# A Mamba block and a router on one core: summing over states by transposes that add in PSUM, with the gate turned instead of the output

## What is computed

```
x  = einsum(ctx, in_proj_w);  u = silu(causal_conv4(x) + conv_b)
dt_low, B, C = split(x_proj_w @ u);  dt = softplus(dt_proj_w @ dt_low + dt_proj_b)
state = state * exp(dt * A) + (dt * u) * B        # step by step over 1024 tokens
y  = sum over 16 states (state * C) + D * u
y  = y * silu(z),  z = layernorm(x), seen as (channel, token)
x2 = x + tanh(g_xattn) * transpose(y)
out = x2 + tanh(g_ffn) * expert_choice_ffn(layernorm(x2))   # one expert matrix, a router of 16
```

## Time and profile before

| | |
|---|---|
| timed runs, us | 2511.08, 2513.67, 2514.60 (median 2513.67) |
| profiled execution, us | 2508.02 |
| its span, us | 2506.2 |
| busy, share of the span | PE 84%, DVE 84%, POOL 80%, ACT 53% |
| granted TensorE clock, mean | 0.922 |

### The profile page before, as it was taken

The page is one execution under the profiler, slowest core; times in us unless marked ns, Lnnn a source line. Parts: engine busy times, 40 slices in busy tenths (PEclk is TensorE's granted clock), DMA queues, the critical chain, the costliest instruction groups (busy, mean ns, idle before and its releaser), DMA issues.

```text
span 2506.2 us, 24916 instructions
## 1 busy us (share of the span) xinstructions
PE 2098.6 (84%) x6072; PEld 1059.0 (42%) x6072; DVE 2103.5 (84%) x2371; ACT 1318.7 (53%) x2269; POOL 2007.3 (80%) x1034
## 2 busy tenths in 40 slices
PE   6597878898888787978888788788878884999998
PEld 2233333343334333333333333333333344678887
DVE  7998999899979998999799989997999874663343
ACT  3556565656566656565656565656565642111111
POOL 0699999999999998999999989999999974122221
PEclk8789998999999998989899989899998995999999
DMA  9501150134113301431143014311431136054441
GB/s 358 189 17 43 40 219 14 55 115 156 31 60 132 135 31 60 149 119 31 60 161 119 30 47 166 110 40 43 168 120 33 49 124 216 9 204 141 150 151 67
DMA packets 74828, 260.55 MB, mean 104 GB/s; under 512 B 8992, under 2 KB 11680, under 8 KB 63552
## 3 DMA queue, kind: packets, MB, share of 16 engines
q1 hardware_dynamic: 74688, 259.01, 29.1%
HBM read 208.05 MB, written 50.92 MB: 103 GB/s over the span
## 4 chain that ended last, share of the span: by engine, by line
POOL 30%; PE 22%; DVE 22%; issue 20%; ACT 4%; DMA 1%; DVEq 1%; POOLq 0%; ACTq 0%; SPq 0%
POOL states L1310 19%; DVE states L1020 11%; PE pDec L740 10%; POOL states L1298 7%; DVE states L1007 4%; PE pY L609 4%; PE pU L740 3%; POOL sp L1279 2%; DVE u L992 1%; PE pA L592 1%; PE pT L652 1%; ACT pDec L834 1%; ACT sz L870 1%; ACT L913 1%; DVE y L1038 1%
## 5 line engine op out<-in xcount | busy, mean ns | idle before, releaser
L609 PE MATMUL pY<-states,con 128*128 128x512 f32 x2048 | 1066.5, 655 | 299.3 <-POOL states L1310 170.8
L1310 POOL TENSOR_TENSOR states<-states,cbc 128x1024 f32<-128x1024 f32 x512 | 1195.5, 2357 | 58.0 <-ACT carry L817 37.2
L834 ACT ACTIVATE pDec<-dt,an 128x512 f32<-128x512 f32 x1024 | 696.9, 689 | 659.9 <-DVE states L1020 654.6
L609 PEld LDWEIGHTS pY<-states,con 128*128 128x128 f32 x2048 | 385.7, 202 | 881.2 <-issue 521.8
L1020 DVE TENSOR_TENSOR_SCAN states<-pDec,carry,states 128x512 f32<-128x512 f32 x512 | 623.3, 1266 | 38.3 <-ACT pDec L834 36.8
L1020 DVE TENSOR_TENSOR_SCAN states<-pDec,states 128x512 f32<-128x512 f32 x512 | 592.5, 1207 | 61.7 <-ACT pDec L834 61.1
L1298 POOL TENSOR_TENSOR states<-dtu,bbc 128x1024 f32<-128x1024 f32 x193 | 455.3, 2359 | 15.7 <-PE pY L609 11.0
L1007 DVE TENSOR_TENSOR states<-pU,bbc 128x1024 f32<-128x1024 f32 x320 | 387.0, 1209 | 11.0 <-ACT pU L812 7.3
L584 PE MATMUL pA<-ctx_sb,win 128*128 128x512 f32 x536 | 245.9, 602 | 7.4 <-DVE u L992 7.4
L1256 DVE TENSOR_TENSOR u<-u,sp 128x1024 f32<-128x1024 f32 x32 | 67.9, 2123 | 169.2 <-ACT u L966 169.2
L966 ACT COPY u<-pDec 128x512 f32<-128x512 f32 x48 | 26.6, 590 | 319.6 <-PE pDec L740 147.5
(11 more groups left out here) (167 smaller groups left out, 2330.5 us busy)
## 6 DMA issues: line engine op xcount, KB each, us to landing
bbc<-bc_scratch SPq DMA_DIRECT2D x35, 1024.0 KB, 4.9
cbc<-bc_scratch SPq DMA_DIRECT2D x34, 1024.0 KB, 5.2
win<-in_winT SPq DMA_DIRECT2D x71, 256.0 KB, 2.7
sz<-in_x SPq DMA_DIRECT2D x16, 1024.0 KB, 5.4
xt<-in_x SPq DMA_DIRECT2D x8, 2048.0 KB, 8.1
x_scratch<-xt SPq DMA_DIRECT2D x8, 2048.0 KB, 6.8
xt<-x_scratch SPq DMA_DIRECT2D x32, 512.0 KB, 4.4
out<-u SPq DMA_DIRECT2D x32, 512.0 KB, 3.0
```

What stands on the lines that cost most here:

```text
L609: mm = pe.matmul(pY[:], ident, states[g % NST][:, i, :], start=(q == 0 and i == 0), stop=(q == QG - 1 and i == QN - 1))
L834: nc.scalar.activation(pDec[turn][:], dt[e % 2][:], ACT.Exp, scale=an[:, k:k + 1]).then_inc(s_dec, 1)
L1310: nc.gpsimd.tensor_tensor(st, st, cbc[:, QN * q:QN * (q + 1), :], ALU.mult).then_inc(s_hc, 1)
```

## The change

- `sum_states`: instead of one product with the identity over 512 columns for each state, four transposes of 128 x 128 for each state, each adding into its quarter of `pY`. The bank then holds y with tokens on the partitions.
- `add_skip` goes; its product (now u against the diagonal, in four pieces of 128 columns) is the first thing written into `pY` in each block, inside `sum_states`. The diagonal holds D*tanh(g), and `low` multiplies the rows of C by tanh(g) (`csc`), so the bank holds tanh(g)*y. The diagonal is made in slot 1 of a block instead of 5.
- `turn_y` and `residual` go. The gate is turned instead: `turn_gate` (four transposes into `pA`, block slot 1) and `gate_out` (ScalarE copies it into `szT`, block slot 2). `inproj` and `xproj`, which also write `pA`, wait for that copy.
- `y_out` multiplies in the bank (`pY<-pY,szT`). A new `add_x` on VectorE, one slot later and behind the first scan of that slot, adds x: `xt<-pY,xt`. The first product of the next block waits for `add_x` where it waited for `y_out`.
- `gate_silu` moves from slots 8 and 40 to 5 and 37, the gates' load from 4 and 36 to 2 and 34, `add_halo` one slot ahead; the load of `xt` from slot 10 to 7, its store from 10 to 5 of the next half; two of the first half's `inproj` one slot later.

```
-SUM of a state:  pe.matmul(pY[:], ident, states[g % NST][:, i, :], ...)
+                 for t in range(TT):
+                     pe.matmul(pY[:, eT(t)], states[g % NST][:, i, eT(t)], ident, start=False, ..., is_transpose=True)
```

```
-HALO_SLOT, SILU_SLOT = [-24], [-23]
+HALO_SLOT, SILU_SLOT = [-25], [-23]
-SKIP_SLOT = [GQ * e + 8 for e in range(E)]
-SZ_SLOT = [8, 40]
+SZ_SLOT = [5, 37]
+SZT_SLOT = [GQ * e + 9 for e in range(E)]
+SZC_SLOT = [s + 1 for s in SZT_SLOT]
 Y_SLOT = [GQ * e + 11 for e in range(E)]
-YT_SLOT = [22, 26] + [GQ * e + 14 for e in range(2, E)]
-RES_SLOT = [s + 3 for s in YT_SLOT]
+X2_SLOT = [s + 1 for s in Y_SLOT]
...
                 if q == 0:
-                    wait(pe, s_y, n(b, o, E, e))
+
+                    wait(pe, s_x2, n(b, o, E, e))
+                    wait(pe, s_diag, n(b, o, E, e + 1))
+                    for t in range(TT):
+                        mm = pe.matmul(pY[:, eT(t)], u[o % 2][:, e, eT(t)], ddiag[:], start=(t == 0), stop=False)
...
-                nc.vector.tensor_tensor(y[e % 2][:], pY[:], sz[:, e % (E // 2), :], ALU.mult).then_inc(s_y, 1)
+                nc.vector.tensor_tensor(pY[:], pY[:], szT[(e + 1) % 2][:], ALU.mult).then_inc(s_y, 1)
+
+            def add_x(b, o, e):
+                wait(dve, s_y, n(b, o, E, e + 1))
+                if e == 0:
+                    wait(dve, s_x, n(b, o, 16, 16))
+                nc.vector.tensor_tensor(xt[:, :, eT(e)], pY[:].rearrange("p (t d) -> p t d", t=TT), xt[:, :, eT(e)],
+                                        ALU.add).then_inc(s_x2, 1)
...
                     for i in range(GN):
                         scan_of(b, o, GN * g + i)
+                        if i == 0:
+                            add_xs(b, o, g, began)
```

More of the change, by code:

```diff
@@ L572, in _, with inproj @@
         def _(pe):
-            def inproj(b, o, j):
+            def inproj(b, o, j, gates):
+                wait(pe, s_szs, gates)
                 if j == 0:
@@ L586, in inproj, with xproj @@
                 mm.then_inc(s_in, 1)
-            def xproj(b, o, part):
+            def xproj(b, o, part, gates):
+                wait(pe, s_szs, gates)
                 if part == 0:
@@ L642, in turn_xf, with logits @@
                 mm.then_inc(s_xfp, 1)
-            def logits(b, o, t, blocks_turned, last=False):
+            def logits(b, o, t, last=False):
                 wait(pe, s_xfT, n(b, o, 2 * TT, 2 * t + 2))
-                wait(pe, s_x2, blocks_turned)
                 wait(pe, s_lga, n(b, o, TT, t))
@@ L662, in side @@
             def side(b, o, g, began):
+                e, ke = latest(SZT_SLOT, g)
+                gates = n(b, o - ke, E, e + 1)
                 for j, k in at_in(0, b, o, g, began):
-                    inproj(b, o - k, j)
+                    inproj(b, o - k, j, gates)
                 for i, k in at(XP_SLOT, g, began):
-                    xproj(b, o - k, i)
+                    xproj(b, o - k, i, gates)
                 for e, k in at(DTP_SLOT, g, began):
@@ L671, in side, with taps_before @@
                 late(b, o, g, began)
+            def taps_before(b, o, g):
+                if isinstance(b, int) and b == 0 and o == 0 and g < IN_SLOT[0] % G:
+                    return HALO * (E + sum(s + G < g for s in IN_FIRST))
+                j, k = latest(IN_SLOT, g)
+                return n(b, o - k, HALO * E, HALO * (j + 1))
             def late(b, o, g, began, least=-9):
[L674 to L676 removed]
                 for i, k in at(SUM_SLOT, g, began):
@@ L789, in low @@
                 wait(act, s_bcw, n(b, o, 16, 0))
-                nc.scalar.copy(xpr[:], bank[0:2 * R, :]).then_inc(s_low, 1)
+                nc.scalar.activation(xpr[:], bank[0:2 * R, :], ACT.Copy, scale=csc[0:2 * R, 2:3]).then_inc(s_low, 1)
             def softplus(b, o, e):
@@ L877, in late @@
             def late(b, o, g, began, least=-9):
-                for e, k in at(RES_SLOT, g, began):
+                for e, k in at(SZC_SLOT, g, began):
                     if k >= least:
-                        residual(b, o - k, e)
+                        gate_out(b, o - k, e)
                 for f, k in at(XFT_SLOT, g, began):
@@ L1113, in late, with add_xs @@
                         softmax_out(b, o - k)
+            def add_xs(b, o, g, began, least=0):
+                for e, k in at(X2_SLOT, g, began):
+                    if k >= least:
+                        add_x(b, o - k, e)
             def half(b, o, began):
```

102 lines of the change are left out of this document (52 added, 50 removed).

## The result

| | before | after |
|---|---|---|
| timed runs, us | 2511.08 to 2521.17, median 2514.14 (4 runs) | 2565.00 to 2570.65, median 2567.36 (4 runs) |
| profiled execution, us; its span | 2508.02; 2506.2 | 2570.65; 2568.8 |
| granted TensorE clock, mean | 0.922 | 0.811 |

The ratio is 1.0216, 95% interval [1.0193, 1.0238]: the changed kernel is 2.2% slower, by 53 us. The forecast was 2586 us, 72 over a kernel of 2514.

What follows compares the result with a forecast made beforehand. VectorE was taken to set the pace, GpSimd a few microseconds behind. Terms 43 - 37 + 4 + 50 + 16 - 4 = +72 us on the profiled 2508.0 made 2580; with 5.7 to the median, 2586 us, range 2497 to 2642.

Steps and rivals of the forecast that it cites:

- Additions, +43: VectorE in the scans: 64 new additions of x at 0.668 us each, +43 us.
- Silu bursts, -37: VectorE's waits for decays behind `silu_u` on ScalarE shrink from 53 to 16 us, -37 us.
- the gates' own wait, +4: VectorE's wait at the gates' silu moves to slots 5 and 37: 16 x 0.3, +4 us.
- -26 for their burst beside the logits wait: In slots 5 and 37 the gates' silu runs beside 13 logits waits, saving 2.0 us each, -26 us.
- Logits at half clock, +91 - 15.5: VectorE's 26 logits reads in the scans wait 3.5 us each, +91 us; the earlier 15.5 us of waits go.
- `xproj`, +16: Bank handed over later inside `xproj`, so ScalarE stands at its copy and delays decays: 2 us per half, +16 us.
- Tail, -4: End of the scans: `turn_y` and `residual` leave the chain, one addition of 0.67 us enters, -4 us.
- The sum over states: TensorE's 512 groups, now transposes, save 1.0 us each, some 500 us of busy time; costed at 0 in the total.
- rival 3: TensorE becomes the bound at half clock: up to 3 us for each of 64 blocks, or 2700 us; chance 0.05.
- Rival 1: TensorE's clock holds or transposes keep it up, so no logits or `xproj` waits: -15, 2499 us; chance 0.22.
- Rival 2: GpSimd is the pace and covers VectorE's additions and waits, leaving nothing of the +72: 2512 us; chance 0.12.
- every microsecond added to VectorE's list counts in full: Reading of the earlier trace: VectorE sets the pace, so its added work lengthens the kernel by the full amount.

Runs made afterwards that it cites:

- the two runs with filling: Changed kernel with six, then ten, products into an unused part of `pT` before TensorE's wait for the bank at each block boundary: 2558.3 and 2538.33 us.
- the table: Scan windows of seven kernels: before, after, and five variants with reads, additions or silu moved or cut; lengths 1958.8 to 2044.4 us.
- both shifts: Changed kernel with the logits read one slot later and x added directly behind the gating: 2493.92 us, in a second run 2490.23 us.

## Why the prediction was right, and where it was off

The direction and the main mechanism held; the time was 2567 where 2586 was forecast. Of these 19 us about half are in the sum, +72 where the spans differ by 62.6. The rest is which executions were profiled: that of before lies 6 us under its median, that of after 3 us over. Two terms were too large and one too small, so that the sum is nearer than some of its parts.

**Additions, +43.** The duration was right (42.5 us in 64), the price was not: VectorE's busy time in the scans rose by 31.5. The mis-sized term is "64 x 0.668". The addition at 1418.10 lasts 0.67 us, but the scan behind it starts at 1418.68, 0.58 later; by start to start 64 are 37 us. The page "Perfetto Trace Analysis" of the Trainium skill, section "Optimizing Scalar/DVE Operations", says so: part of a profiled duration overlaps with the next instruction. The trace agrees (0.67 and 0.58 us). The other 6 us are not the additions'. In the same windows three kinds of small piece that the change leaves alone took 9.0 us less (`cur<-ln` 11.7 and then 6.7 us, `lg<-lg,mx` 10.6 and 8.5, `S_tok<-lg,rc` 4.8 and 3.1), and the window of after takes in some 3 us more at its end. `cur<-ln`, eight instructions of 128 x 16, lasted 0.60 to 2.30 us before and 0.26 to 1.64 after; no run says why.

**Silu bursts, -37, the gates' own wait, +4, and -26 for their burst beside the logits wait.** Together -59; the decay waits fell by 56.6. Behind `silu_u` 2.8 and 1.2 us were forecast for first and second halves and 1.93 and 1.65 measured. The term has the right size for this pair of kernels, and the run that undid it gives 56. It isn't the move's own worth: on the kernel before it gave 20 us, since there the gates' burst has no logits wait to hide under. Whether GpSimd has a part in the difference is not shown.

**Logits at half clock, +91 - 15.5.** Forecast: chain of 10.8 us at half clock and a wait of 5.3; measured 10.88 and 5.7 to 6.05. Forecast mean wait 3.5, two thirds of the full one; measured 106.2 / 26 = 4.1. The net is +91 where I had +75.5. At full clock I had 5.5 us for the chain and no wait; the two runs with filling show 5.7 to 6.1. The waits are 0.6 to 0.9 where TensorE stood for the hand-over, and 1.2 to 2.9 where the filling itself made it late.

**`xproj`, +16.** Too large. ScalarE stands at the copy for up to 2.8 us, but VectorE's wait behind it went from 3.8 to 8.7 us in seven halves, some +5.

**Tail, -4.** From the end of the window of the scans to the end of the span 448.8 us before, 445.7 after: -3.1.

In the scans the terms other than the additions were to give -37 + 4 + 50 + 16 = +33, and VectorE's idle time rose by 33.6: too little for the logits and too much for `xproj` cancel, which is luck. With the additions at their measured 31.5 and the tail, +62, which is the difference of the spans (62.6). The medians differ by 53 us, since the profiled execution of before (2508.02) lies below all its timed runs and that of after is its slowest.

**Readings that do not follow from their rows.** The sum over states was to save TensorE some 500 us; it is busy 308 us less, and much of what is left runs at half clock, where eight transposes take 1.97 us instead of 1.09. In the earlier trace rows TensorE lacks 15% of the window, not 17%. And rival 3's own numbers, 28 + 4 us against 30.8, make 1.2 us for each block or 77 in all, not 3 and 2700. None of these carries the sum.

**Rival 1** (transposes keep the clock up) failed: 0.79 in the scans, no chain at full clock from its start. What the clock did is more than either side said, though. In the windows at 596 to 626 us TensorE is busy without a gap for 7 us, with sums, the `dtproj` of 32 rows and logits products of 16 columns, and stays at half clock. Then come 40 transposes and nothing else:

```profile
596.56 2.07 PE L611 MATMUL pD<-xpr,dtp 32*128 32x512 f32 x2
598.56 1.97 PE L625 MATMUL pY<-con,states 128*128 128x128 f32 x8
600.32 3.43 PE L660 MATMUL pT<-rw,xfT 128*128 128x16 f32 x16
...
603.59 7.18 PE L625 MATMUL pY<-con,states 128*128 128x128 f32 x40
610.61 0.60 PE L635 MATMUL pA<-con,sz 128*128 128x128 f32 x4
```

and after 5.2 us of them the clock is full. So the rule of the Trainium skill ("TensorE: Matmul & The Clock Gate", Part 4, PE-mode transpose) that full clock does not engage for the transpose mode is contradicted for these FP32 transposes: they alone brought it back. That the clock falls where TensorE stands for the bank is shown by the filling. Why it then stays low is not. In 14 chains it came back 2.8 to 4.6 us after the chain's start, in the 12 others only 15.2 to 16.4 us after it, when the logits were done. All of them hold the 32-row and 16-column products, and what share these have was not tried by themselves.

**Rival 2** (GpSimd covers VectorE) was wrong for the change as made. With the logits wait GpSimd stood still 143.6 us of the scans, without it 76.0. As soon as that wait is gone, VectorE's work is covered for the most part, as the rival said, but only in part by what the rival named. The claim "every microsecond added to VectorE's list counts in full" fell: of 31.2 us taken off VectorE, 6 to 13 show, and 42.5 us more on it cost 7. My reading of the earlier trace rows took the engine with the larger waits for the pace and GpSimd "a few microseconds behind". GpSimd's busy time fills the scans to within 63 to 76 us in every kernel of the table that is faster than before, VectorE's to within 89 to 126, and VectorE's longest waits there are for ScalarE's decays. No run shows one engine that sets the pace alone.

**Rival 3** (TensorE as the bound) did not come: 1348 us busy of 2044.

The three parts of the change, then: the silu move is worth 20 us on its own. The transposes, the turned gate and the additions cost 7 us even with both shifts in place, where they are measured against the best arrangement of the kernel before (its gates' burst in slots 6 and 38, not 5 and 37). And 69 us were lost to one instruction left in the slot where it used to be in time. The fastest kernel of the study is the kernel before with the silu move and the logits read one slot later (2483.3 us); the changed kernel with its read moved (2498.33) also beats the kernel before.

## What to carry over

When a change hands a buffer over later, list every fixed-slot read downstream of it and compare its slack with the producer's chain at the slow clock as well as at the full one; moving such a read by one slot was worth 69 us here, more than any other single edit. Price an added VectorE instruction by start-to-start distance, not by duration, and price it a second time against the waits in which the engine stands anyway (here for ScalarE's bursts) and against the engine that fills the stage (GpSimd here): of the time taken off VectorE less than half showed. And measure the parts of a compound change on the kernel before as well: two waits that hide each other gave 56 us one way and 20 the other.

## What was not expected of the hardware

- FP32 transposes of 128 x 128 count for the clock: after 5.2 us of them alone it went from 0.50 to 1.00 (windows from 603.60 us), while it had stayed at 0.50 through the 7 us of unbroken work just before, which held 32-row and 16-column products too.
- With six filling products, the clock was full for 5.5 us or the whole chain where TensorE had stood 1.4 to 2.4 us before it. After 3.0 to 4.6 us it was at half at the start or fell to it within 1.2 us.
- The transposing mode is one record for FP32 where a plain product is two: 1.09 against 2.05 us for eight of 128 columns at full clock.
- Using PSUM as input and output of one VectorE multiplication cost no more than writing SBUF: 674 against 668 ns.
